# Graph attention kernel: a small input with the samples of the sorted edge list, and a new order of the first loads and of the weight preparation

## The reference, cut to what matters

```python
def gat_layer(x, src, dst, W, a_src, a_dst, b, n_nodes):
    h = x @ W
    s = h @ a_src
    d = h @ a_dst
    e = leaky_relu(s[src] + d[dst], 0.2)
    m = segment_max(e, dst, n_nodes)
    ex = exp(e - m[dst])
    z = segment_sum(ex, dst, n_nodes)
    alpha = ex / z[dst]
    return segment_sum(alpha[:, None] * h[src], dst, n_nodes) + b

h = maximum(layernorm(x), 0)
x = x + gat(relu(gat(h, W1, ...)), W2, ...)     # first block
h = maximum(layernorm(x), 0)
x = x + gat(h, W3, ...)                         # second block
```

## Time and profile before

| | us |
|---|---|
| median of 3 runs | 767.15 |
| lowest and highest | 763.31, 767.67 |
| the profiled execution, its own time | 764.39 |
| its span, first to last instruction | 762.7 |

### The profile page before, as it was taken

How to read it: one execution, slowest core, us unless ns; L and a number is a source line. 1 busy time by engine, 2 the same in 40 slices (tenths; PEclk the granted TensorE clock), 3 DMA queues, 4 the chain that set the end, 5 groups by cost and what they waited for, 6 DMA issues and landing times.

```text
span 762.7 us, 14382 instructions
## 1 busy us (share of the span) xinstructions
PE 652.2 (86%) x5581; PEld 634.2 (83%) x5581; DVE 693.6 (91%) x903; ACT 506.3 (66%) x739; POOL 372.1 (49%) x344
## 2 busy tenths in 40 slices
PE   3219889899876999999999989999979989998994
PEld 3119889888865989999989989998979889998984
DVE  1699998999987999999998899999997989999994
ACT  1015463545537987879776689788776789697880
POOL 3130000000044555646485567677588767785873
PEclk9968897989886999999999999999999999999998
DMA  3500000000002232222133233222123223323211
GB/s 82 133 3 2 1 1 1 1 1 2 1 7 22 80 106 90 74 79 75 34 70 104 100 63 109 85 72 76 36 66 84 82 65 83 108 92 118 77 56 39
DMA packets 50015, 45.38 MB, mean 60 GB/s; under 512 B 13328, under 2 KB 47865, under 8 KB 49940
## 3 DMA queue, kind: packets, MB, share of 16 engines
q1 hardware_dynamic: 49140, 43.13, 19.9%
q0 software_dynamic: 800, 1.26, 0.6%
HBM read 31.33 MB, written 13.05 MB: 58 GB/s over the span
## 4 chain that ended last, share of the span: by engine, by line
PE 27%; DVE 23%; issue 8%; DMA 5%; ACT 3%; POOL 3%; DVEq 0%; SPq 0%; POOLq 0%
PE ps L1673 22%; DVE ps L941 11%; DVE scratch L1019 6%; DVE ps L943 2%; DMA g_lines<-g_row 1%; POOL scratch L657 1%; DVE mu L953 1%; ACT scratch L1423 1%; PE ps L1726 1%; DMA scratch<-counts_bf 1%; DMA gathered<-g_lines 1%; PE ps L1704 1%; PE ps L1681 1%; ACT scratch L1369 1%; ACT scratch L1429 1%
## 5 line engine op out<-in xcount | busy, mean ns | idle before, releaser
L1673 PE MATMUL ps<-hB,scratch 125*125 125x129 f32 x3450 | 405.5, 276 | 29.1 <-DVE scratch L1019 22.6
L1673 PEld LDWEIGHTS ps<-hB,scratch 125*125 125x125 f32 x3450 | 391.0, 189 | 38.4 <-DVE scratch L1019 30.2
L657 POOL TENSOR_TENSOR scratch<-scratch 125x625 f32<-125x625 f32 x197 | 262.0, 1338 | 151.4 <-ACT scratch L1429 133.0
L941 DVE SCALAR_TENSOR_TENSOR ps<-C,a_unit,ps 125x625 f32<-125x625 uint8 x330 | 277.3, 865 | 2.1
L1429 ACT ACTIVATE scratch<-scratch,r_src 125x625 f32<-125x625 f32 x197 | 178.4, 905 | 4.7
L1423 ACT ACTIVATE scratch<-gathered,r_inv 125x625 f32<-125x625 f32 x197 | 159.1, 808 | 31.7 <-PE ps L1673 25.0
L1604 PE MATMUL ps<-scratch 128*128 128x125 bf16 x1250 | 148.4, 296 | 19.6 <-issue 10.5
L1604 PEld LDWEIGHTS ps<-scratch 128*128 128x128 bf16 x1250 | 143.4, 120 | 23.6 <-DVE scratch L852 12.4
L1019 DVE SCALAR_TENSOR_TENSOR scratch<-ps,r_src,C 125x625 f32<-125x625 f32 x178 | 152.9, 859 | 8.9 <-PE ps L1657 8.9
L1299 ACT ACTIVATE C<-ps 125x1750 uint8<-125x1750 f32 (+3 forms) x50 | 74.3, 1489 | 108.7 <-PE ps L1604 108.7
L852 DVE TENSOR_TENSOR scratch<-key_col,hB 128x6500 bf16<-128x6500 bf16 (+3 forms) x26 | 92.9, 3572 | 0.0
(11 more groups left out here) (161 smaller groups left out, 415.9 us busy)
## 6 DMA issues: line engine op xcount, KB each, us to landing
scratch<-counts_bf SPq DMA_DIRECT2D x142, 152.6 KB
counts_bf<-scratch SPq DMA_DIRECT2D x73, 152.6 KB
gathered<-g_lines SPq DMA_DIRECT2D x14, 305.2 KB
xr<-in_x SPq DMA_DIRECT2D x1, 1562.5 KB
out<-xr SPq DMA_DIRECT2D x5, 312.5 KB
edge_sb<-in_edges SPq DMA_DIRECT2D x1, 805.7 KB
gathered<-ext_lines SPq DMA_DIRECT2D x5, 122.1 KB
w<-in_W SPq DMA_DIRECT2D x2, 128.0 KB
```

Of the source, the lines that this page charges most:

```text
L657: g.tensor_tensor(slot[s], slot[s], wide[r % WIDE], ALU.mult).then_inc(pool_done, 1)
L941: v.scalar_tensor_tensor(dest, counts, unit[:, s:s + 1], top, ALU.min, ALU.max).then_inc(S.top_done, 1)
L1673: last = mm(ps[0:P, acc_at(t):acc_at(t) + HW], A[:, P * t:P * (t + 1)], feat, start=opens and t in (0, 3), stop=closes, skip_group_check=True)
```

## The change: what it does

1. There is a new input, `apart`: the destinations, [125, 25, 33] in the order of the list, transposed on the host to [33, 125, 25] and laid out contiguously. Its first plane, `apart[0]`, holds the 125 x 25 samples, 12.5 KB. SP loads it first, in place of the edge list, into the new tile `sample_i` with the same semaphore `edges_in`. DVE's L783 copies from it.
2. SP loads x after `first_in` (the first gather has landed), no longer after `starts_ok`.
3. The edge list is loaded last of the inputs, after `gather_in` (all gathers) and `x_in`. SP then waits for it to land, ahead of its L478. DVE waits for it only in `general_counts`, on the slow path.
4. On PE the transposes of the first keys stand ahead of the preparation of the weights, and on ACT `copy_keys(0)` does.

```diff
-            sp.dma_start(edge_sb[:, :, :], edges.rearrange("(p k) c -> p k c", p=P)).then_inc(edges_in, 16)
+            sp.dma_start(sample_i[:, :], apart[0, :, :]).then_inc(edges_in, 16)
             sp.dma_start(w1[:, :], W1).then_inc(weights_in, 16)
...
-            sp.wait_ge(starts_ok, 1)
+            sp.wait_ge(first_in, 16)
             sp.dma_start(xr[:, :, :], x_v).then_inc(x_in, 16)
+            sp.wait_ge(gather_in, 16 * (WG - 1))
+            sp.wait_ge(x_in, 16)
+            sp.dma_start(edge_sb[:, :, :], edges.rearrange("(p k) c -> p k c", p=P)).then_inc(edges_in, 16)
+            sp.wait_ge(edges_in, 32)
...
             dve.wait_ge(edges_in, 16)
-            v.tensor_copy(sampled[:, :], edge_sb[:, :, :].rearrange("p (k r) c -> p k r c", r=SAMPLE)[:, :, 0, 1]
-                          ).then_inc(start_lin, 1)
+            v.tensor_copy(sampled[:, :], sample_i[:, :]).then_inc(start_lin, 1)
...
             def general_counts():
                 dve.wait_ge(flag_ok, 1)
+                dve.wait_ge(edges_in, 32)
...
             a_.activation(steps[:, 0:NS], ps[0:P, DIF:DIF + NS], ACT.Copy).then_inc(steps_sb, 1)
 
+            def copy_keys(g):
...
+            copy_keys(0)
+
             act.wait_ge(prep_T, 1)
...
             last.then_inc(before_sum, 1)
 
+            for i, key in enumerate((k_lo, k_hi)):
+                pe.wait_ge(keys_ok, i + 1)
+                for k in range(KC):
+                    n = KEYS0[i] + 128 * k
+                    last = tr(ps[0:128, n:n + P], key[:, 0, 128 * k:128 * (k + 1)], ident[0:P, 0:P])
+                last.then_inc(keys_T, 1)
+
             pe.wait_ge(weights_in, 16 * N_WEIGHTS)
...
             pe.wait_ge(prep_done, 1)
-            for i, key in enumerate((k_lo, k_hi)):
...
+        "apart": inputs["dst"].reshape(125, 25, 33).transpose(2, 0, 1),
```

More of the change, by code:

```diff
@@ L5, with gat_stack_kernel @@
 from concourse import mybir
-def gat_stack_kernel(nc, x, edges, W1, a_src1, a_dst1, b1, W2, a_src2, a_dst2, b2,
+def gat_stack_kernel(nc, x, edges, apart, W1, a_src1, a_dst1, b1, W2, a_src2, a_dst2, b2,
                      W3, a_src3, a_dst3, b3, out):
@@ L101, in gat_stack_kernel @@
         sampled = sb("sampled", [P, NS])
+        sample_i = sb("sample_i", [P, NS], i32)
         win_base = sb("win_base", [P, WG])
@@ L1262, in _ @@
             a_.activation(steps[:, 0:NS], ps[0:P, DIF:DIF + NS], ACT.Copy).then_inc(steps_sb, 1)
+            def copy_keys(g):
+                for i, (key, minus) in enumerate(((key_lo, 0.0), (key_col, -1.0))):
+                    act.wait_ge(keys_T, 2 * g + (2 if g else i + 1))
+                    a_.activation(key[:, g, 0:P, :].rearrange("p w k -> p k w"),
+                                  tiles((KEYS_AT if g else KEYS0)[i], KC, rows=128), ACT.Copy, bias=minus).then_inc(keys_sb, 1)
+            copy_keys(0)
             act.wait_ge(prep_T, 1)
@@ L1272, in _ @@
             a_.activation(w3[:, D:AW], ps[:, VEC + 6:VEC + 8], ACT.Copy).then_inc(prep_done, 1)
[L1274 to L1280, removed]
             def normalise_first(c):
```

## The result

| | before | changed |
|---|---|---|
| median | 765.74 us (8 runs) | 759.95 us (8 runs) |
| lowest and highest | 763.31, 767.67 | 758.0, 762.35 |
| profiled execution, own time | 764.39 | 762.35 |
| its span | 762.7 | 760.5 |

The ratio is 0.9932, with a 95% interval of 0.9915 to 0.9948: some 5.2 us faster, clear of noise and under 1%. The forecast was 760.9, in a range of 756.5 to 766.5. The profiled execution of the changed kernel is the slowest of its eight, that of before lies in the lower part of its own; the two profiles differ by 2 us only.

A forecast was written before the change was run, and what follows sets the result against it. DVE's instruction string was taken to bound the count stage. Samples 6.5 us plus first gather 3.0 minus 4.8 idle for x gave 4.7 us gained, from a base of 765.6 to 760.9 us; range 756.5 to 766.5.

The forecast's parts named there:

- The bound: Count stage: a string of DVE instructions limits it, so a microsecond saved ahead of it moves the end by one.
- The samples: Head: a 12.5 KB load replaces 805.7 KB, samples there at 3.7 us, starts at 8.45; 6.5 us won up to the gather.
- The first gather: Head: with no x beside it, it takes 6.5 us and lands at 16.1 instead of 25.6; another 3.0 us won.
- the 4.7: Head: total gain in us at the start of the statistics of x, 37.75 instead of 42.42.
- x: Load of x, issued at 16.15, takes 21.2 us, still losing 3.3 to later gathers; DVE idles 4.8 us before the statistics.
- The 2.7 us that the prediction has beside the sum: Load of x: by the engine rule, the last two gathers cost it 2.7 us instead of 3.3; x there 0.6 earlier.
- x meets no gather: Rival on x's load: x takes 17.9 us, statistics start at 34.4, 8.0 us won, 757.6; chance 0.14.
- The first gather's time is its own: Rival: its 9.5 us come of being first, not of x; 1.7 us won, 763.9; chance 0.12.
- x moved past too much: Slower rival: x, issued behind the first gather, still needs 23.86 us; 1.0 us lost, 766.6; chance 0.08.
- 2.6 us for this gather: Rival from the skill's rule on the first gather: statistics start at 33.8, 8.6 us won, 757.0; chance 0.04.
- The rest: Weight preparation order on PE and ACT, and the edge list loaded last: both hidden, the order worth nothing either way.
- 1 us of either sign: TensorE's clock: a shifted pattern at the first products, where the level matters, may be worth this much.

The follow-up runs named there:

- e1: Changed kernel with x issued once the starts are known, not behind the first gather: 762.62 us, ratio 0.9954 to the kernel before.
- e6: Changed kernel without the load of the edge list: 758.23 us, ratio 0.9904 to the kernel before.
- e8: Changed kernel with nine more statistics instructions on DVE behind the real ones, 1.8 us of delay: 760.02 us, ratio 0.9944 to the kernel before.
- e5: Kernel before with only x moved behind the first gather, whole edge list still loaded first: 764.66 us, ratio 0.9996 to the kernel before.
- e3: Changed kernel with x issued only after all five gathers have landed: 763.45 us, ratio 0.9958 to the kernel before.
- e2: Changed kernel with the weights prepared ahead of the first keys again on PE and ACT: 760.57 us, ratio 0.9915 to the kernel before.
- e4: Changed kernel with x loaded in two transfers, of 112 and 13 partitions: 755.61 us, ratio 0.9861 to the kernel before.
- e7: Changed kernel with x in two transfers right behind the samples and DVE's node statistics ahead of the first keys: 750.52 us, ratio 0.9819 to the kernel before.

## Why the prediction was right, and where it wasn't

**The bound: right.** What comes before DVE's string goes to the end of the count stage, to within 2 us: from the start of the statistics to the extremes it is 177.4 us before, 176.6 in the changed kernel, and 176.6 to 178.5 in e1 to e6. In e8 the 1.8 us of delay come out as 1.9.

**The samples: right in sum, out in two parts that cancel.** I had them at 3.7, bounded by 3.15 and 4.2; they are there at 2.48. The lower bound was misread: the copy doesn't wait for POOL's constants, the compare behind it (L791) does, and it starts at 3.25. And the chain that "the change leaves alone" didn't stay as it was: from the compare to `start_i` it takes 8.24 - 3.25 = 4.99 us, 4.53 before (14.96 - 10.43). The compare itself takes 1.38 us in every kernel with the samples in place and 0.55 in the kernel before and in e5. It has moved beside an instruction of POOL (3.09 to 4.29), which is the likely reason and wasn't tested:

```profile
3.09 1.20 POOL L598 IOTA hB<- 128x512 bf16 x1
```

```profile
10.43 0.55 DVE L787 TENSOR_SCALAR scratch<-hA,sampled 125x625 f32<-125x625 f32 x1
```

The first line is of the changed kernel, the second is the compare of the kernel before. The starts came at 8.24 instead of 8.45. The 1.12 us up to the first gather stood.

**The first gather: mis-sized.** 6.5 us forecast, with a lower bound of 6.2; it took 5.7, and the later ones as little as 4.2. The bound was wrong because all five rows of before were of gathers with x beside them: the fastest of them wasn't one without x. This is 0.8 us of the 1.6 by which the head came out better than the 4.7; 0.2 are of the starts, 0.5 of x.

**x: right in kind, a little long.** The new idle time was forecast at 4.8 us and measured at 4.14, x from issue to statistics at 21.6 and measured at 21.1. What was left of the collision is 2.8 us, by e3, where the sum had 3.3. x alone, 18.3 us by e3, is the 17.9 + 0.4 of the lower bound. The 2.7 us that the prediction has beside the sum, by the Trainium skill, DMA: Bandwidth & Descriptors, section "Why a DMA increments its semaphore by 16 and not by 1", are nearer to the 2.8; but by its reading the last two gathers meet x, and the fourth took 4.6 us, 4.4 in e3 with no x, so the trace doesn't bear out which ones collide. Reading the two holes in the earlier trace rows as collisions was right; e1 shows it from the other side.

**The rivals.** "x meets no gather" is out: e3 shows what that looks like, 18.3 us. "The first gather's time is its own" is out for the 9.5 us, by e1 and by its 5.7 us; some of it is its own, since in e3, with no x near, the first takes 5.6 us and the next ones 4.2. The slower one, x moved past too much, has the right mechanism: in e5, with x issued at 21.6, the gain is nil. The prediction put its turning point at 18.2, with x at its whole 23.86 us. With the 21.2 us of an x that is spared the first gather it would have been 42.42 - 0.4 - 21.2 = 20.8; e5 puts it at 21.7. The rule of the Trainium skill, DMA: Bandwidth & Descriptors, section "Anatomy of one DMA — SWDGE (gpsimd) path", gives 2.6 us for this gather; the trace disagrees with it for this kind of transfer, with 5.7 us for the first and none under 4.1 in any run.

**The rest: free, as said.** The order on PE and ACT (e2) and the list (e6, up to the extremes).

**Behind the extremes: the term that was too small.** I gave the clock "1 us of either sign" and nothing else. The head gave 6.3 us to the statistics and 7.1 to the extremes; the profiled execution kept 2.2 of it at its end, so 4.9 us were given back. The longer low stretch of the clock in the second layer is 2.3 of them, by the windows above. Nearly all of the rest comes with the clock at its upper level in both profiles: 1.2 us between the load at 406.91 and the store at 431.69 (L478 and L483), which takes 24.8 us in the changed kernel and 23.6 in the kernel before (413.83 to 437.39), and 1.4 us between the store of extremes at 610.44 and the first store of `out` at 649.63, 39.2 against 37.8 us (613.94 to 651.69). The first of these two appears in six of the ten profiles (the changed kernel, e2, e3, e5, e6 and e8). I have found no cause for either; both stay open.

In the medians less is lost: 5.2 (by the ratio) to 5.8 us of the 6.3 to 7.1 remain. That the forecast of 760.9 was so near to 759.95 is in part two errors that cancel: 1.6 us too little at the head, and 0.5 to 1.9 us given back behind it for which the sum had no term.

## What to carry to other kernels

Before a load is moved behind another, work out when its reader will want it, and how long it takes alone: here the reader was 4 us early, and what the change won from the samples and the gather together (10.5 us to the first keys) it could keep only up to x's landing. Look at the number of partitions of a large load: splitting the one over 125 in two, of 112 and 13, by the rule on divisors named under e4, was worth 4.3 us here. And idle time on the engine that bounds the next stage is the place for its independent work: issuing x first and moving 6.6 us of statistics there brought 4.2 us more (14.4 us gained over the kernel before, 10.2 with the split alone), as much as the split and more than the new place of x (2.7).

## What the runs showed of the hardware that I had not expected

- A gather of 251 KB took 5.7 us with no x beside it, and 12.9 us with the 1.6 MB load of x, in rows of 512 bytes, issued 1.1 us ahead of it; that load took 29 us beside five such gathers, and 18.3 alone.
- One transfer over 125 partitions moved its 512-byte rows at 99 GB/s; two, over 112 and 13, at 252 GB/s with the weights among them, but at 132 beside the gathers. The last of the gathers took up to 12.4 us then, 9.4 in the changed kernel.
- The issue of x's second transfer kept SP busy for 4.78 us in e4 and 3.49 us in e7, where most other issues take 0.3 to 0.5.
- The same pause of PE, 0.9 us of work in 3.4 us, was followed by 6.8 us at the lower granted clock in the changed kernel, 3.4 us in e5 and none in the kernel before, and the last two reach it at the same time. A change of 2 us in such a kernel can't be read from one profile of each.
